# A two-pass graph layer on one core: the far cells of the next stripe loaded one stripe ahead, and each column step moved behind up to five cells of other work

## The reference

```python
def _L0_gnn_ref(x, adj, W):
    A_hat = adj + jnp.eye(adj.shape[0], dtype=adj.dtype)
    d_inv_sqrt = jnp.sum(A_hat, axis=1) ** (-0.5)
    A_norm = d_inv_sqrt[:, None] * A_hat * d_inv_sqrt[None, :]
    support = x @ W.T
    out = A_norm @ support
    return jax.nn.relu(out)
h = jnp.maximum(_layernorm(x, axis=-1), 0.0)
x = x + _L0_gnn_ref(h, adj, L0_gnn_W)
```

## Time and profile before

| | before |
|---|---|
| median of 3 runs | 1205.84 us (1203.95 to 1207.55) |
| the profiled execution: its span, which is its time here | 1237.8 us |
| PE busy | 983.2 us (79%) |
| DVE busy | 802.4 us (65%) |
| ACT busy | 586.5 us (47%) |
| moved by DMA | 391.81 MB, mean 317 GB/s |

### The profile page before, as it was taken

One profiled execution on the slowest core, in us unless ns is written; L12 is line 12 of the kernel. 1 busy time (PEld: TensorE's weight loads), 2 busy tenths in 40 slices (PEclk: granted clock), 3 DMA queues, 4 the chain that ended last, 5 costly groups with the idle time before them and its releaser, 6 DMA issues.

```text
span 1237.8 us, 9242 instructions
## 1 busy us (share of the span) xinstructions
PE 983.2 (79%) x2365; PEld 451.8 (36%) x2365; DVE 802.4 (65%) x965; ACT 586.5 (47%) x1735; POOL 52.6 (4%) x61
## 2 busy tenths in 40 slices
PE   0633346566687788796597999999999999899997
PEld 0631122222233333342243444444444444344443
DVE  5342233444476566575485888888888888778775
ACT  2797587776384637145254451724715653010011
POOL 3000000000000000000000000000000000010001
PEclk9767668678889899998798999999999999999999
DMA  9989999999999999999999999999999997999993
GB/s 301 380 320 309 392 398 362 365 369 347 362 349 343 362 337 322 314 256 274 281 291 278 329 332 360 323 276 333 309 325 320 314 271 215 271 271 348 337 328 88
DMA packets 275204, 391.81 MB, mean 317 GB/s; under 512 B 10832, under 2 KB 252624, under 8 KB 275152
## 3 DMA queue, kind: packets, MB, share of 16 engines
q1 hardware_dynamic: 137648, 195.65, 51.3%
q10 hardware_dynamic: 137504, 195.58, 50.5%
HBM read 386.99 MB, written 4.19 MB: 316 GB/s over the span
## 4 chain that ended last, share of the span: by engine, by line
PE 37%; DMA 8%; ACT 6%; ACTq 3%; DVE 1%; issue 0%; POOLq 0%; SPq 0%; DVEq 0%
PE bank L485 36%; DMA slot<-in_adj_dram 8%; ACT junk L540 6%; ACTq L269 2%; DVE adjT L692 1%; ACTq L277 1%; PE pre L461 0%; ACTq L315 0%; DVE near L778 0%; ACT slot L530 0%; ACT near L558 0%; DVE part L677 0%; POOLq L175 0%; PE sums_bank L449 0%; ACTq L321 0%
## 5 line engine op out<-in xcount | busy, mean ns | idle before, releaser
L485 PE MATMUL bank<-adjT,support 128*128 128x512 f32 x2048 | 936.2, 618 | 152.1 <-DVE adjT L692 150.8
L692 DVE STREAM_TRANSPOSE adjT<-slot 128x1024 f32<-128x1024 f32 x450 | 546.5, 1233 | 268.8 <-DMA slot<-in_adj_dram 157.2
L485 PEld LDWEIGHTS bank<-adjT,support 128*128 128x128 f32 x2048 | 401.8, 199 | 664.6 <-issue 661.0
L540 ACT ACTIVATE junk<-slot 128x384 bf16<-128x384 f32 (+2 forms) x540 | 254.6, 473 | 196.1 <-issue 131.3
L530 ACT ACTIVATE slot<-slot 128x6144 f32<-128x6144 f32 (+11 forms) x64 | 191.8, 2998 | 250.3 <-issue 147.8
L558 ACT ACTIVATE near<-near,dinv 128x128 f32<-128x128 f32 x64 | 20.4, 390 | 177.9 <-issue 88.5
L540 ACT ACTIVATION_READ_ACCUMULATOR junk<-slot 128x1 f32 x540 | 100.8, 187 | 0.0
L692 DVE STREAM_TRANSPOSE adjT<-near 128x1024 f32<-128x1024 f32 x62 | 74.8, 1231 | 19.0 <-PE bank L485 19.0
L540 ACT ACTIVATE junk<-near 128x256 bf16<-128x256 f32 (+1 forms) x192 | 75.5, 394 | 2.8 <-ACT junk L540 2.8
L677 DVE TENSOR_REDUCE part<-slot 128x4 f32<-128x1536 f32 (+2 forms) x45 | 69.0, 1533 | 0.0
L407 POOL TENSOR_TENSOR dinv<-total,power 128x4 f32<-128x4 f32 x16 | 16.1, 1007 | 942.0 <-DVE total L746 942.0
(11 more groups left out here) (53 smaller groups left out, 179.1 us busy)
## 6 DMA issues: line engine op xcount, KB each, us to landing
slot<-in_adj_dram SPq DMA_DIRECT2D x118, 768.0 KB, 15.4
slot<-in_adj_dram ACTq DMA_DIRECT2D x118, 768.0 KB, 13.4
slot<-in_adj_dram ACTq DMA_DIRECT2D x56, 512.0 KB, 11.0
slot<-in_adj_dram SPq DMA_DIRECT2D x56, 512.0 KB, 12.0
slot<-in_adj_dram ACTq DMA_DIRECT2D x12, 1536.0 KB, 15.8
slot<-in_adj_dram SPq DMA_DIRECT2D x12, 1536.0 KB, 17.0
near<-in_adj_dram SPq DMA_DIRECT2D x30, 512.0 KB, 16.8
near<-in_adj_dram ACTq DMA_DIRECT2D x30, 512.0 KB, 15.2
```

The lines of the kernel that those rows point to most:

```text
L485: ins = nc.tensor.matmul(bank[bank_of(g)][:], support[:, v * R + t, :], adjT[at % TURNS][:, r, :], start=(n == first_of[g] and t == 0), st ...
L540: nc.scalar.activation(junk[at % JUNKS][:, :n], cells[:, c, :], ACT.Copy, accum_out=part[u % 2][:, k, c:c + 1]).then_inc(junk_done, 1)
L692: nc.vector.transpose(adjT[at % TURNS][:].rearrange("p t (c i) -> p t c i", i=Q), half.rearrange("p c (t r) -> p t c r", r=Q)).then_inc(t_ ...
```

## The change

It reorders two lists and what follows them. First, `landing` has per stripe s: left, near, then the far pieces of stripe s+1 in one block, then the again pieces of s. ACT follows this list (`stream`). Stripe 0 has its own far pieces in front, as before. For stripes 0 to 4, which have no again pieces, the list of loads is the same as before.

Second, in `order` the column of stripe s stands behind up to five cells (LEAD = 5) of what can be done without it: again cells of s first, then left cells of stripe s+1, though of the latter at most s (those whose scale exists). So column(1) stands behind one left cell of stripe 2, column(2) behind two of stripe 3, column(3) behind three of stripe 4, column(4) behind four of stripe 5, and from stripe 5 on behind five cells. DVE folds the sums two cells into these, makes the totals three cells in, and scales support four cells in. `far_sum` gets a third buffer. The number of DMAs, products and sums is the same.

```diff
-    for u in range(NB):
+    for u in range(NB):
+        stream[u], left[u], early[u] = [], [], []
+        if u == 0:
+            for piece_ in far_pieces(0):
+                place_piece(0, piece_)
+        own = [("left", u, v, n, 0, 0) for v, n in split(0, u)] + ["near"]
         if u <= EARLY_TO:
...
+            own += [("again", i, u - MOST, MOST, 0, 0) for i in range(u - MOST - BAND - 1, -1, -MOST)]
+        ahead = far_pieces(u + 1)
+        done = 0
+        for k, piece_ in enumerate(own):
+            if piece_ == "near":
+                near_behind[len(landing) - 1] = u
+                stream[u].append("near")
+            else:
+                place_piece(u, piece_)
+            upto = len(ahead) if piece_ == "near" else done
+            for piece_ in ahead[done:upto]:
+                place_piece(u, piece_)
+            done = upto
...
     for s in range(NB):
+        lefts, behind = todo[s]
+        order += lefts[ready:]
+        following = todo[s + 1][0][:s] if s + 1 < NB else rest[:LEAD]
         stripe_at[s] = len(order)
-        own = [(landing[m][1], v, m) for m in left[s] + early[s] for v in range(landing[m][2], landing[m][2] + landing[m][3])]
-        before = 0 if NB - 1 - s - BAND > 4 else min(FIRST, max(0, s - 1))
-        order += own[:before]
-        if s > 0:
-            column(s - 1)
-        order += own[before:]
+        begun = behind[:LEAD]
+        ready = min(len(following), LEAD - len(begun))
+        order += begun + following[:ready]
+        column(s)
+        order += behind[LEAD:]
+        if s + 1 == NB:
+            order += rest[ready:]
...
-        far_sum = [sb(f"far_sum{i}", [P, 2 * B]) for i in range(2)]
+        far_sum = [sb(f"far_sum{i}", [P, 2 * B]) for i in range(3)]
...
             for m in range(AGAIN):
                 load_piece(sp, (0, 1), m)
-                if m in last_piece:
-                    load_kept(sp, (0, 1), last_piece[m])
+                if m in near_behind:
+                    load_kept(sp, (0, 1), near_behind[m])
...
+            for n in range(len(order)):
+                if folds < NB and n == min(stripe_at[folds] + 2, column_at[folds]):
+                    fold_sums(folds)
+                    folds += 1
+                product(n)
...
+                fold_at.setdefault(min(stripe_at[s] + 2, column_at[s]), s)
+                totals_at.setdefault(min(stripe_at[s] + 3, column_at[s]), s)
+                scale_at.setdefault(min(stripe_at[s] + 4, column_at[s]), s)
```

More of the change, by code:

```diff
@@ L47, in gnn_kernel @@
     DVE_C = 4
-    FIRST = 4
+    LEAD = 5
     JUNKS = 3
@@ L82, in gnn_kernel, with far_pieces @@
     landing = []
-    far, left, again, early = {}, {}, {}, {}
+    far, left, again, early, stream = {u: [] for u in range(NB)}, {}, {}, {}, {}
+    near_behind = {}
     next_cell = [u + BAND + 1 for u in range(FAR_ROWS)]
     middle = []
-    for u in range(NB):
+    def far_pieces(u):
         cells = NB - 1 - u - BAND
-        far[u] = []
         widths = [] if cells <= 0 else [cells] if cells <= MOST * B else [MOST * B, cells - MOST * B]
+        out_ = []
         for k, width in enumerate(widths):
@@ L91, in gnn_kernel @@
             per = min(B, MOST * B // width)
-            for bb in range(0, B, per):
-                far[u].append(len(landing))
-                landing.append(("far", u, bb, min(per, B - bb), NB - cells + k * MOST * B, width))
-        left[u] = []
-        for v, n in split(0, u):
-            left[u].append(len(landing))
-            landing.append(("left", u, v, n, 0, 0))
-        early[u] = []
-        if u <= EARLY_TO:
-            for i in range(u - MOST - BAND - 1, -1, -MOST):
-                early[u].append(len(landing))
-                middle.append((i, u - MOST))
-                landing.append(("again", i, u - MOST, MOST, 0, 0))
-                next_cell[i] = u
+            out_ += [("far", u, bb, min(per, B - bb), NB - cells + k * MOST * B, width) for bb in range(0, B, per)]
@@ L339, in done_by @@
             return sum(combined_at(k) + 1 < place[u, v + n - 1] for k in range(NB))
-        last_piece = {(far[u] + left[u])[-1]: u for u in range(NB)}
         @block.sync
@@ L487, in product @@
                     ins.then_inc(used, 1)
[L489 to L501 removed]
+            back = folds = 0
+            for n in range(len(order)):
[3 more added lines that the diff above has]
+                product(n)
+                if back < NB and n >= 4 + last_final(back):
+                    rows_back(back)
+                    back += 1
             while back < NB:
```

145 lines of the change are left out of this document (73 added, 72 removed).

## The result

The changed kernel takes **1315.46 us** (median of 4 runs, 1312.80 to 1323.41), the kernel before 1206.69 us beside it on the same chip: a ratio of 1.0921, interval 1.0873 to 1.0968. That is 109 us slower. The forecast said slower, +48 us, and its range ended at 1274 us: the sign is right, the size is not.

A forecast was written before the change was run, and what follows sets the result against it. Loads pace the kernel until PE reaches cell 101, then products take a fixed rest. Near-load waits of 45 us plus 12.5 of restarts, 57, less 9 at stripe 10, give +48: 1254 us, range 1216 to 1274.

The forecast's parts named there:

- the sum of the dry spells: Stripes 2 to 7: DMA engines run dry before near loads, 45 us of waits and 12.5 from issue to data, 57 us.
- the term for the column at stripe 9: Near load of stripe 10: its 9.2 us wait goes, winning 9 us.
- the spells are waits and not rates: Whole kernel: the difference of +48 us in the profiled span carries over unchanged to the median.
- What bounds the kernel: Loads set the pace until PE reaches cell 101, then a fixed rest; delaying all earlier loads by d costs about d.
- Far cells one stripe ahead: Far and again pieces change places from stripe 5 on, at no cost, since only total bytes count in the DMA-bound stage.
- The wait for the near load: Stripes 2 to 7: near load waits for a column behind pieces in flight, ACT and SP stand, DMA runs dry; 57 us.
- From issue to data: After each dry spell, time until data flow again: 2.5 us, bounds 0 and 2.7, counted five times, 12.5 us.
- the 64 KB row: Profile row of the smallest transfer, 2.7 us from issue to landing, taken as nearest to the restart cost.
- Half filled in: Rival: DMA runs faster after dry spells, regaining 20 us in the early stripes, +28 us, 1234 us; chance 0.22.
- Faster: Rival: from 506 to 683 us column and near-load order holds loads back; the change saves 25 us, 1181 us; chance 0.08.
- Worse: Rival: DVE waits in the fold for ACT's near sums, 5 us in each of stripes 8 to 13, 1284 us; chance 0.04.
- What would show it: Signs: early stretches 55 to 60 us, DMA share near 0.8, near load issued in 1.5 us, last PE idle near 725.

The follow-up runs named there:

- e8: The changed kernel with the order of loads of the kernel before, far pieces behind again pieces, columns still late: 1314.35 us.
- e11: The changed kernel with fold, totals and scale of stripes 1 to 6 in front of the cells that the column stands behind: 1302.58 us.
- e6: The changed kernel with SP alone, not ACT, loading the near cells of stripes 2 to 7: 1273.34 us.
- the second execution: The kernel before, unchanged, profiled once more: span 1203.7 us against 1237.8 in its first profile; measured time 1205.53 us.
- e9: The changed kernel with the loads of the kernel before and left cells in front of a column only from stripe 9 on: 1231.64 us.

## Why the prediction was wrong in size

The step that failed is the sum of the dry spells, +57 us: 97 us of DMA time went unfilled. With it failed the term for the column at stripe 9, -9 us, of which nothing came, and the assumption that the spells are waits and not rates, which was short by the 13 us of longer packets.

**What bounds the kernel.** Right. What is lost early comes out at the end nearly unchanged: 107.8 us at stripe 8, 109 at the end.

**Far cells one stripe ahead, cost 0.** Right for the total, within what a run can tell: with the loads of before (e8) the time is the same.

**The wait for the near load, 57 us.** Right in place and kind, too small. Term by term:

- Stripe 2: 9.0 predicted, 12.5 measured (155.29 to 167.81). Stripe 3: 13.0 against 16.6. The missing 3.5 us is PE's product in front of its sums. I took fold to scale from 130.69 to 134.91, where PE had nothing in front; now DVE waits 4.69 and 4.86 us there, against 1.13 where nothing is in front (e11, 193.90). The product was slow as well: eight matmuls in 5.76 us, at a granted clock of 0.50 (1.2 GHz) after 38.78 us of idle time, where a cell takes 3.445 at the full clock.
- Stripes 4 and 5: counted from the first left piece, 9.0 and 10.3 plus the 7.4 us between pieces, 16.4 and 17.7. Measured 15.7 (282.11 to 297.80) and 17.6 (342.94 to 360.57). These were right.
- Stripes 6 to 8: 3, 0.5 and 0 predicted, 7, 5 and 2.5 us of dry engines measured.
- From issue to data: 2.5 predicted. The engines were dry 15 and 20 us where the first two waits were 12.5 and 16.6, so 2.5 and 3.4 us. This was nearly right. The section that the prediction names beside it (the Trainium skill, DMA: Bandwidth & Descriptors, Anatomy of one DMA) is on DMAs issued from GpSimd, while the 64 KB row is one of SP's; no run here isolates that cost.
- Sum of dry time before the near loads: 57 us predicted, 71 us read from the windows.

**What was left out behind the near load.** The prediction ended each loss when the near load was issued plus 2.5 us. But ACT had stood in that wait, and all its sums came behind it. The slots that those sums hold are what the next pieces need, so the next pieces were issued one by one at ACT's pace (174.91 to 203.46). The text had the facts: ACT stands in the wait itself, and it works 31 to 34 us of each stretch of 43 to 47. I used that row only to show that ACT had time to spare. In a stretch in which it does nothing for 33 us it has none: 33 + 32 = 65 us, and the stretch measured 67 us. What this costs is smaller than that sum suggests. Behind the first dry spell the DMA engines are full while ACT catches up (1.11, 1.02, 1.02 and 1.02 from 170 to 210 us), and the pieces follow each other at the same pace as before. Only in the later stretches are there dips, 10 us in all. The 42 us that came back with ACT out of the wait (e6) are not a term beside the dry spells: they are dry time that went, since ACT then fed the engines during the wait.

**The account.** Predicted: 57 - 9 = 48. Between the profiled executions: 97 us not filled and 13 of longer packets, 109.5. Of the 97, 71 stand before the near loads and 10 in the dips; the other 16 are not assigned to a place by any run; a part of them is that the spells are read against a share of 1.00 and this account against 1.028. So some 40 of the missing 61 us are unfilled time, 13 are packets and 9 are the gain that did not come, each rounded.

**What each dry spell leaves behind.** Also missing: slower packets, 13 us over the whole execution. The windows at 234 to 252 GB/s stand where they may come from, but no run isolated it. e6 has more of it (100.4% of 1263.8 us, 1269 us of packets), with less dry time.

**The column at stripe 9 and after, -9 us.** The wait was read rightly, 9.19 and 9.15 us in the two executions, and it is gone in the change: ACT's issue before it runs to 689.91, and the near load follows at once.

```profile
666.46 23.45 ACTq L280 DMA_DIRECT2D slot<-in_adj_dram  x6
690.02 5.14 ACTq L326 DMA_DIRECT2D near<-in_adj_dram  x2
```

The near load of stripe 10 is 101.1 us late where that of stripe 8 was 107.8, but at the end 109 us are lost, so none of it was kept. What failed there is to price the wait by the stall behind it: in the second execution the DMA engines stay full through the wait and PE's stall is 5.34 us. This sets the sum 9 us too low.

**The rivals.** "Half filled in" fell: behind a dry spell DMA is not faster (247 GB/s at a share of 1.11), and the packets took 13 us more in all. "Faster" fell with the dry spells of 11 to 20 us. "Worse", that DVE stands in the fold for ACT, is not what happened in the changed kernel, where such waits total 6 us, but it is real where loads are on time: the 34 us from stripe 8 on in e9. It had the range's missing direction, for another reason than the true one, and I gave it 4%. The range was built from bounds on each wait, and none on what a longer wait does to the engine that stands in it. The bounds as stated, added up, give about 1229 to 1276 and not 1236 to 1272; the measured time lies far outside either.

**What would show it.** The near load's 1.5 us, the gaps on ACT and the share (0.74 to 0.83) came as said. The stretches grew to 63 to 67 and not 55 to 60. That was the sign in the text's own terms that the sum was too small. The wait at the near load of stripe 10 is gone, as said. The last idle time came at 730.02 against 725, but 583 us from the end and not 561, so at an earlier cell; cell 101 is at about 1313.2 - 561 = 752.

## What to carry to other kernels

Before moving work in front of a buffer's last use, ask which load waits for that use, and who issues it. A load that reuses a buffer should wait for work that is done before the last outstanding piece lands: one cell of a late piece in front of each of four columns cost 63 us, up to four cost 77. And where the engine that stands in such a wait also computes and issues the next loads, the wait empties the queues behind it: with another engine in the wait 42 of 109 us came back. A check of the total is the page's share of the load queues times the span, before and after: what it leaves over is DMA time that nobody filled, and here it showed 97 us where the waits one by one gave 71.

## What the runs showed of the chip

- A full DMA share does not mean a full rate: 1.11 with 247 GB/s in the 10 us behind a dry spell, 1.02 with 417 a window later.
- The same two near issues take ACT 1.54 us at a DMA share of 0.07 (167.81, the change) and 10.36 us where loads are in flight (138.60, the kernel before). But a short issue is no sign of dry engines: at 588.88 in the second execution it took 1.55 us at a share of 1.07.
- Two executions of one kernel differed by 28 us in one stage (from the near load of stripe 8 to that of stripe 10, 141.8 us against 169.9) with nothing changed: 352 GB/s at a share of 1.07 against 296 at 1.05. A gain read from one such stage needs a second profile.
